# A four-layer graph network on one core: layer 2 in 128-row groups written out, layer 0 without zeroed weight buffers

## The chip, the cores and the metric

The kernel runs on one core of one Trainium2 chip. The metric is the device time of one execution in microseconds; three runs of the kernel before gave a median of 2008.88 us (2003.04 to 2011.71).

## What is computed

3125 nodes with 256 features, 53125 edges sorted by destination (25000 random pairs in both directions and a loop on every node). Four layers, each followed by a residual and a layer norm over the features:

```python
edge_index = jnp.stack([src, dst])
x = _layernorm(x + _L0_gnn_ref(x, edge_index, W, b), axis=-1)                  # relu(sum of h[src] * dinv[src] * dinv[dst] + b), h = x @ W
x = _layernorm(x + _L1_gnn_ref(x, edge_index, edge_weight, ...), axis=-1)      # (sum of x[src] * w) @ W_rel.T + b_rel + x @ W_root.T
x = _layernorm(x + _L2_gnn_ref(x, W, att, src, dst), axis=-1)                  # attention, 4 heads of 64
x = _layernorm(x + _L3_gnn_ref(x, edge_weight, W, b, src, dst), axis=-1)       # relu(sum of (x @ W)[src] * w + b)
```

Layer 2 in full:

```python
z = jnp.einsum('nd,hdf->nhf', h, W)
es = jnp.einsum('nhf,hf->nh', z, a_src)
ed = jnp.einsum('nhf,hf->nh', z, a_dst)
e = jax.nn.leaky_relu(es[src] + ed[dst], SLOPE)
e = jnp.where(e == 0.0, NEG, e)
m = jax.ops.segment_max(e, dst, num_segments=N)
ex = jnp.exp(e - m[dst])
denom = jax.ops.segment_sum(ex, dst, num_segments=N)
alpha = ex / safe
out = jax.ops.segment_sum(alpha[:, :, None] * z[src], dst, num_segments=N)
```

## The kernel before, in words

Nodes lie in 25 tiles of 128. The kernel is written engine by engine: each of SP, POOL (GpSimd), ACT, DVE and PE has its own list of instructions, and semaphores with counts set the order between them.

**Start.** SP loads destinations, sources and weights of the edges, x and the matrices, and last the destinations once more in the grouping of layer 2 (dst_i, L310). DVE packs the edges into a table of six bf16 fields; SP stores it in DRAM (edge_list, L313) and spreads it to overlapping rows (edge_rows, L317). DVE also counts degrees, finds for each group of layer 2 its lowest node and, from the widest group, how many sweeps layer 2 needs (nsw, one here); TensorE's first products of x wait for that (L742, L1119). ACT scales them (L471), once the edge list is stored, since the results take its place.

**Layer 0** also builds the adjacency matrices that layers 1 and 3 use. For every tile t of sources, 32 panels of destinations lie on 32 partitions with 128 edges each. POOL (edge_rows) gathers the panels' rows from edge_rows by an indirect DMA (L413), moves the cursor (L417) and marks edges of another panel (L419, L422). TensorE turns the five fields (turn_fields, L1144), ACT copies them in two halves (digits, L489), DVE makes one-hots of them (one_hot_lo L775, one_hot_code L778) and multiplies them by three bf16 parts of the weight (weighted, L783). TensorE makes from them, in eight quads (adjacency), counts (L1157) and weights (L1160). ACT evicts the counts (L493); DVE adds each quad of weights to the weight buffer aw[t % 2] (add_weights, L796). The buffer holds zeros before: POOL wrote them (L427) after the store of tile t-2 (a_stored), and DVE waits for that (c_zero). SP stores the finished buffer to DRAM (L324). Then TensorE multiplies the counts with the scaled features (aggregate, L1168), and the residual parts of the tiles before are done: sums0 (L812, L815), the norm (L800, L801, L498, L805, L806), the turning of the normalised tile (L1177) and the two products of layer 1 (L1186). The number of rounds per tile (nswb) is read at run time; it is one here. The program of one tile has the turning of the next fields between the fourth and the fifth quad. DVE makes the next tile's one-hots between its additions 4 to 7, in an order written out by hand.

**Layer 1** loads the stored matrices (four slots) and makes dense products (L1224), and the rows of the attention table: per node 268 floats, z with a one behind each head and both logits. SP stores them in DRAM (L346, L349).

**Layer 2** goes over groups of edges. A group is EP x KC = 125 x 5 edges: 85 groups, taken five at a time (SLOTS) in a loop of 17 turns; the first and the last turn are written out apart. Per group: SP loads the source indices (L361) once the slot of the ring is free, and the destination logits of a window of 48 nodes (L367); POOL gathers five times 125 rows of the attention table by indirect DMAs (L450), five groups ahead at most. DVE makes one-hots of the destinations within the window (L901, L906), TensorE turns them (L1255), multiplies them by the window's logits (L1264), DVE forms the logits (L912 to L931), masks them to the window (L938), takes the maximum over the five edges of a partition (L946); TensorE turns that (L1273), DVE takes the maximum over the partitions (L951), puts it on a diagonal (L957), TensorE spreads it to all partitions (L1281), DVE updates the running maximum (L966, L972, L982) and shifts the logits (L977), ACT takes the exponentials (L568, L571), TensorE sums the gathered rows by window (L1290, 40 small products a group), DVE rescales and adds (L990, L998). The parts of neighbouring groups are interleaved by hand: in one step DVE masks group k, prepares k+1 and k+2 and finishes k-1 and k-2. Windows start at a base that each engine loads into a register (base_i); a turn of the loop loads anew the bases of the groups that it touches.

**Layer 3** multiplies by its matrix (L1354) and makes the dense products with the stored matrices again.

## Time and profile before

| what | us |
|---|---|
| median of 3 runs | 2008.88 (2003.04 to 2011.71) |
| the profiled execution, its own time | 2004.1 |
| its span, first to last instruction | 2002.2 |
| around the span | 1.9 |
| TensorE busy | 1748.5 (87%) |
| DVE busy | 1274.0 (64%) |
| POOL busy | 673.2 (34%) |
| ACT busy | 449.5 (22%) |
| mean granted clock of TensorE | 0.81 of full speed |

A share of the whole span is an average over stages with different limits, so the stages are read one by one: layer 0 lasts from about 110 us to 615 us of the span, layer 1 to 940, layer 2 to 1631, layer 3 to the end. Instructions are named by their line of the kernel before; "idle before" names the time in which the engine stood still ahead of an instruction, and what ended it ("issue": nothing that the profile shows). PEld is TensorE's weight load, which overlaps its products.

### The profile page before, as it was taken

What the parts mean: (1) busy time and instruction counts of PE and PEld (TensorE: products, weight loads), DVE (VectorE), ACT (ScalarE), POOL (GpSimd) and SP (SyncE); (2) the same over time, 40 slices, a digit from 0 to 9 for tenths busy, and PEclk for the clock granted to TensorE, in tenths of its full rate; (3) what the DMA queues carried; (4) which work ended last, traced back from release to release, by engine and by line L of the source; (5) the groups of instructions that cost most, each with busy time, mean ns of one, the idle gap of its engine ahead of it and who ended that gap; (6) DMA issues with size and microseconds to landing.
All of it is one profiled execution on the core that took longest, in us unless ns stands there. A gap on an engine that the chain in (4) does not pass through costs nothing.

```text
span 2002.2 us, 38284 instructions
## 1 busy us (share of the span) xinstructions
PE 1748.5 (87%) x13533; PEld 1503.9 (75%) x13533; DVE 1274.0 (64%) x2915; ACT 449.5 (22%) x1000; POOL 673.2 (34%) x567
## 2 busy tenths in 40 slices
PE   5668898888888999996689889998988877899998
PEld 5457777767776888885578778887877765788887
DVE  9678888888885112222788888888898876311212
ACT  0432322222321001002233332332333333100000
POOL 0122222222222000001777777777777800000000
PEclk9989999999999999998555555555555555899999
DMA  6102121212124344441333333333333330245441
GB/s 168 70 36 102 70 102 70 102 70 102 70 103 197 108 143 143 151 146 45 91 91 83 89 86 88 86 85 89 86 89 88 90 114 1 97 151 176 162 157 45
DMA packets 110199, 202.38 MB, mean 101 GB/s; under 512 B 70372, under 2 KB 87061, under 8 KB 100483
## 3 DMA queue, kind: packets, MB, share of 16 engines
q1 hardware_dynamic: 54851, 141.62, 20.1%
q0 software_dynamic: 55232, 59.15, 12.3%
q8 instruction: 80, 1.31, 0.3%
q14 instruction: 36, 0.29, 0.0%
HBM read 152.00 MB, written 53.36 MB: 103 GB/s over the span
## 4 chain that ended last, share of the span: by engine, by line
PE 57%; issue 23%; DVE 8%; DMA 4%; POOL 4%; ACT 2%; DVEq 1%; POOLq 0%; SPq 0%; ACTq 0%
PE bank L1224 27%; PE bank L1290 16%; PE bank L1281 4%; DMA ring<-edge_rows,cur 3%; PE bank L1264 2%; PE bank L1354 2%; POOL ring L450 2%; PE bank L1273 1%; PE bank L1232 1%; POOL ring L419 1%; DVE work L957 1%; PE bank L1177 1%; PE bank L1337 1%; ACT ring L593 1%; DMA ring<-attention_rows,work 1%
## 5 line engine op out<-in xcount | busy, mean ns | idle before, releaser
L450 POOL DMA_INDIRECT ring<-attention_rows,work x425 | 514.8, 1211 | 172.9 <-issue 143.4
L1290 PE MATMUL bank<-work,ring 125*65 125x48 f32 x3400 | 395.1, 302 | 0.0
L1290 PEld LDWEIGHTS bank<-work,ring 125*65 125x65 f32 x3400 | 387.7, 224 | 8.4
L1224 PE MATMUL bank<-big,ring 128*128 128x256 f32 x1250 | 273.0, 379 | 1.4 <-DVE x_sb L821 1.4
L1224 PE MATMUL bank<-big 128*128 128x256 f32 x1250 | 272.9, 379 | 0.0
L1224 PEld LDWEIGHTS bank<-big,ring 128*128 128x128 f32 x1250 | 236.5, 190 | 33.8 <-DVE x_sb L821 2.2
L1224 PEld LDWEIGHTS bank<-big 128*128 128x128 f32 x1250 | 236.6, 190 | 31.7
L1168 PE MATMUL bank<-big 128*128 128x256 bf16 x1875 | 209.0, 273 | 14.6 <-ACT big L493 14.6
L1168 PEld LDWEIGHTS bank<-big 128*128 128x128 bf16 x1875 | 181.4, 98 | 38.9 <-ACT big L493 18.3
L427 POOL MEMSET big<- 128x3200 f32 x25 | 69.2, 2770 | 355.3 <-DMA adjacency<-big 295.2
L1157 PE MATMUL bank<-work 128*128 128x100 bf16 x800 | 153.5, 210 | 33.4 <-DVE big L796 28.8
L1160 PE MATMUL bank<-work 128*128 128x100 bf16 x2400 | 164.5, 210 | 0.0
L1160 PEld LDWEIGHTS bank<-work 128*128 128x128 bf16 x2400 | 151.1, 99 | 0.2
L946 DVE TENSOR_REDUCE work<-work 125x192 f32<-125x960 f32 x85 | 150.9, 1776 | 0.0
L783 DVE TENSOR_TENSOR work<-work,ring 128x1600 bf16<-128x1600 bf16 x156 | 149.3, 985 | 0.0
L498 ACT ACTIVATE std<-mv,epsc 128x1 f32<-128x1 f32 x100 | 29.5, 295 | 527.7 <-DVE mv L801 527.7
L1281 PE MATMUL bank<-work,ones 96*128 96x192 f32 x170 | 82.7, 588 | 72.9 <-DVE work L957 72.9
L1053 DVE TENSOR_TENSOR u<-bank,bias 128x256 f32<-128x256 f32 x25 | 10.6, 424 | 211.1 <-PE bank L1224 211.1
L796 DVE TENSOR_TENSOR big<-big,bank 128x400 f32<-128x400 f32 x200 | 113.4, 567 | 23.5 <-PE bank L1160 23.4
L493 ACT CAST big<-bank 128x400 bf16<-128x400 f32 x200 | 98.5, 492 | 120.9 <-PE bank L1160 120.9
L1157 PEld LDWEIGHTS bank<-work 128*128 128x128 bf16 x800 | 78.7, 98 | 44.9 <-DVE big L796 36.0
L1281 PEld LDWEIGHTS bank<-work,ones 96*128 96x128 f32 x170 | 41.2, 301 | 94.0 <-DVE work L957 94.0
(204 smaller groups left out, 2153.8 us busy)
## 6 DMA issues: line engine op xcount, KB each, us to landing
adjacency<-big SPq DMA_DIRECT2D x25, 1600.0 KB, 5.2
ring<-adjacency SPq DMA_DIRECT2D x25, 1600.0 KB, 7.0
big<-adjacency SPq DMA_DIRECT2D x25, 1600.0 KB, 7.2
ring<-attention_rows,work POOLq DMA_INDIRECT x425, 3.9
edge_rows<-edge_list SPq DMA_DIRECT2D x1, 4983.0 KB
x_sb<-in_x SPq DMA_DIRECT2D x1, 3072.0 KB
out_x<-xnT SPq DMA_DIRECT2D x24, 128.0 KB, 4.3
attention_rows<-ring SPq DMA_DIRECT2D x13, 135.0 KB, 2.3
```

The source lines that it names most:

```text
L427: G.memset(aw[t % 2], 0.0).then_inc(c_zero, 1)
L450: G.indirect_dma_start(out=rows[0:EP, s, c, 0:ZG], out_offset=None, in_=ztab[:, :], in_offset=bass.IndirectOffsetOnAxis(ap=idx[:, s, c:c + ...
L493: S.copy(ac[:, :, q * QUAD * PAN:(q + 1) * QUAD * PAN], cnt_banks[q % 2][:, 0:NT * QUAD * PAN].rearrange("p (b d) -> p b d", b=NT)).then_i ...
L783: ins = V.tensor_tensor(oh[h][2][:, j], oh[h][1], repeated(digs[h][:, W1 + j], NT * PAN), ALU.mult)
L796: V.tensor_tensor(part, part, w_banks[q % 2][:, 0:NT * QUAD * PAN].rearrange("p (b d) -> p b d", b=NT), ALU.add).then_inc(c_wad, 1)
L946: V.tensor_reduce(vmax[:], val[:, three(s)].rearrange("p c w -> p w c"), AX_X, ALU.max).then_inc(y["vmax_ready"], 1)
L1157: mm(cnt_banks[b][:, 0:NT * QUAD * PAN].rearrange("p (b d) -> p b d", b=NT)[:, :, cols], lo[:, g, :, m], code[:, g, :, m].rearrange("p (b ...
L1160: ins = mm(w_banks[b][:, 0:NT * QUAD * PAN].rearrange("p (b d) -> p b d", b=NT)[:, :, cols], lo[:, g, :, m], wtd[:, j, g, :, m].rearrange( ...
L1168: ins = mm(out_banks[t % 2][:, 0:D], ac[:, b, :], y0p[:, b, j, :], start=False, stop=False, skip_group_check=True)
L1224: ins = mm(bank[:, 0:D], slots[s][:, b, :], ybuf[:, b, :], start=(b == 0), stop=(b == NT - 1))
L1281: mm(mb_bank[:, 0:HW], ones[0:2 * WIN, :], dg[:].rearrange("p k w -> p (k w)"), start=True, stop=True).then_inc(y["mb"], 1)
L1290: ins = mm(sum_banks[three(s)][0:FH, h * WIN:(h + 1) * WIN], rows[0:EP, s, c, h * FH:(h + 1) * FH], prob[:, s % 2, c, h * WIN:(h + 1) * WI ...
```

## The change

Layer 0: POOL zeroes the two weight buffers once (t < 2) and no more. Every addition is a scalar_tensor_tensor: old content times a column of keep, plus the new quad; the column is 0 for the first round of a tile and 1 for others. DVE, and no more POOL, waits for the store of the buffer two tiles back. Addition 5 stands ahead of one_hot_lo, and the later additions and products move accordingly.

Layer 2: groups have 128 x 5 = 640 edges. 83 are full, the 84th has the last five edges; its empty rows have a destination of 1e30, no one-hot, and source 0, and the search for bases and sweeps ignores them (a few more DVE operations). No loop over turns: all 84 groups are written out on all five engines, and buffers that went by slot % 2 with an exception for the fifth go by group number % 3 and % 2. SP copies all source indices at the start from DRAM to DRAM into the layout of the groups (source_nodes) and loads them at once in layer 1, ahead of the fourth matrix; POOL waits for that one load and for the slot. SP has the window loads only.

```diff
@@ sizes @@
-    EP = max(p for p in range(1, P + 1) if E % (p * KC * SLOTS) == 0)
-    GROUPS = E // (EP * KC)
-    TURNS = GROUPS // SLOTS
+    EP = P
+    FULL = E // (EP * KC)
+    GROUPS = FULL + 1
+    REST = (E - FULL * EP * KC) // KC
@@ SP, start @@
-            sp.dma_start(dst_i[:], dst.rearrange("(g p k) -> p g k", p=EP, k=KC)).then_inc(ld_dsti, 16)
+            sp.dma_start(dst_i[:, 0:FULL, :], dst[0:FULL * EP * KC].rearrange("(g p k) -> p g k", p=EP, k=KC)).then_inc(
+                ld_dsti, 16)
+            sp.dma_start(dst_i[0:REST, FULL, :], dst[FULL * EP * KC:E].rearrange("(p k) -> p k", k=KC)).then_inc(ld_dsti, 16)
+            sp.dma_start(src_all[:, 0:FULL, :], src[0:FULL * EP * KC].rearrange("(g p k) -> p g k", p=EP, k=KC)).then_inc(
+                s_srcs, 16)
+            sp.dma_start(src_all[0:REST, FULL, :], src[FULL * EP * KC:E].rearrange("(p k) -> p k", k=KC)).then_inc(s_srcs, 16)
+            sp.dma_start(src_all[REST:EP, FULL, :], spare[REST:EP, :]).then_inc(s_srcs, 16)
@@ SP, layer 1 @@
+                elif t == 3:
+                    sp.wait_ge(s_srcs, 48)
+                    sp.wait_ge(c_quad, nswb * (QUADS * NT))
+                    sp.sem_inc(held, 1)
+                    sp.dma_start(idx, src_all).then_inc(idx_ready, 16)
@@ SP, layer 2 @@
-                with sp.Fori(0, TURNS) as q:
-                    for s in range(SLOTS):
-                        i = r * GROUPS + q * SLOTS + s
-                        sp.wait_ge(y["slot_free"], i + 1)
-                        sp.dma_start(idx[:, s, :], src_v[:, bass.ds(q * SLOTS + s, 1), :].rearrange(
-                            "p a k -> p (a k)")).then_inc(idx_ready[s], 16)
-                        sp.wait_ge(z_stored[0], 16 * (NT - NT // 2))
-                        sp.wait_ge(z_stored[1], 16 * (NT // 2))
-                        base = sp.value_load(base_i[0:1, bass.ds(q * SLOTS + s, 1)], min_val=0, max_val=NPAD - WIN)
-                        sp.wait_ge(y["ed_ps"], i + 1)
-                        sp.dma_start(edw[:, s, :], ztab[bass.ds(base, WIN), ED:ZG]).then_inc(edw_loaded[s], 16)
+                for g in range(GROUPS):
+                    s = g % SLOTS
+                    base = sp.value_load(base_i[0:1, g:g + 1], min_val=0, max_val=NPAD - WIN)
+                    sp.wait_ge(y["ed_ps"], r * GROUPS + (g + 1))
+                    sp.dma_start(edw[:, s, :], ztab[bass.ds(base, WIN), ED:ZG]).then_inc(edw_loaded[s], 16)
@@ POOL, layer 0 @@
-                if t >= 2:
-                    pool.wait_ge(a_stored[t % 2], 16 * (t // 2))
-                G.memset(aw[t % 2], 0.0).then_inc(c_zero, 1)
+                if t < 2:
+                    G.memset(aw[t % 2], 0.0).then_inc(c_zero, 1)
@@ POOL, layer 2 @@
+            pool.wait_ge(idx_ready, 16)
             with pool.Fori(0, nsw) as r:
-                with pool.Fori(0, TURNS) as q:
-                    for s in range(SLOTS):
-                        pool.wait_ge(idx_ready[s], 16 * (r * TURNS + q + 1))
-                        pool.sem_inc(held, 1)
+                for g in range(GROUPS):
+                    s = g % SLOTS
+                    pool.wait_ge(y["slot_free"], r * GROUPS + (g + 1))
+                    pool.sem_inc(held, 1)
@@ DVE, start @@
-            dve.wait_ge(ld_dsti, 16)
-            link(V.tensor_copy(dstf[:], dst_i[:]))
+            dve.wait_ge(ld_dsti, 32)
+            V.tensor_copy(dstf[:, 0:FULL, :], dst_i[:, 0:FULL, :])
+            link(V.tensor_copy(dstf[0:REST, FULL, :], dst_i[0:REST, FULL, :]))
             V.tensor_reduce(gmin[:], dstf[:], AX_X, ALU.min)
-            V.tensor_reduce(gmax[:], dstf[:], AX_X, ALU.max).then_inc(s_gm, 1)
+            link(V.scalar_tensor_tensor(out=within, in0=dstf[:], scalar=BIG / 2, in1=dstf[:], op0=ALU.is_lt, op1=ALU.mult))
+            link(V.tensor_scalar(gmin[:], gmin[:], float(N), None, ALU.min))
+            V.tensor_reduce(gmax[:], within, AX_X, ALU.max).then_inc(s_gm, 1)
@@ DVE, layer 0 @@
-                V.tensor_tensor(part, part, w_banks[q % 2][:, 0:NT * QUAD * PAN].rearrange("p (b d) -> p b d", b=NT),
-                                ALU.add).then_inc(c_wad, 1)
+                V.scalar_tensor_tensor(out=part, in0=part, scalar=keep[:, bass.ds(r, 1)],
+                                       in1=w_banks[q % 2][:, 0:NT * QUAD * PAN].rearrange("p (b d) -> p b d", b=NT),
+                                       op0=ALU.mult, op1=ALU.add).then_inc(c_wad, 1)
-                    dve.wait_ge(c_zero, t + 1)
+                    if t < 2:
+                        dve.wait_ge(c_zero, t + 1)
+                    else:
+                        dve.wait_ge(a_stored[t % 2], 16 * (t // 2))
-                        add_weights(t, i, 4)
+                        add_weights(t, i, 4, r)
+                        add_weights(t, i, 5, r)
                         one_hot_lo(0)
-                        add_weights(t, i, 5)
+                        add_weights(t, i, 6, r)
                         weighted(i + 1, 0, 0)
-                        add_weights(t, i, 6)
-                        weighted(i + 1, 0, 1)
-                        add_weights(t, i, 7)
-                        weighted(i + 1, 0, 2)
+                        add_weights(t, i, 7, r)
+                        for j in range(1, 3):
+                            weighted(i + 1, 0, j)
@@ DVE, layer 2; ACT and PE alike @@
-                attention_turn(r, 0, first=True)
-                with dve.Fori(1, TURNS - 1) as q:
-                    attention_turn(r, q)
-                attention_turn(r, TURNS - 1, last=True)
+                attention(r)
```

## Rows read from the trace of the kernel before

**Rows 1.** Chain that ended last, 100 to 600 us: two of 24 gathers' landings.

```profile
139.13 2.38 DMA ring<-edge_rows,cur
...
580.90 2.38 DMA ring<-edge_rows,cur
```

**Rows 2.** Timeline of a tile of layer 0: start us, us, engine, line, idle before it.

```profile
197.22 2.76 POOL L427 MEMSET big<- 128x3200 f32 x1 [13.15 <-DMA adjacency<-big]
...
198.90 1.22 DVE L806 TENSOR_SCALAR x_sb<-u,mv,rstd 128x256 f32<-128x256 f32 x1
...
204.04 0.49 ACT L493 CAST big<-bank 128x400 bf16<-128x400 f32 x1 [0.24 <-PE bank L1160]
...
204.72 0.37 PE L1144 MATMUL bank<-ident,ring 32*128 32x32 bf16 x5 [0.72 <-POOL ring L422]
...
205.57 0.99 DVE L778 TENSOR_TENSOR work<-ring 128x1600 bf16<-128x1600 bf16 x1 [0.96 <-ACT ring L489]
...
219.17 0.51 DVE L806 TENSOR_SCALAR x_sb<-u,mv,rstd 128x256 f32<-128x256 f32 x1
```

**Rows 3.** TensorE's waits, 100 to 600 us (waited for: us in total, times, longest us).

```profile
PE bank L1144 <- POOL ring L422: 18.8, 23, 2.4
```

**Rows 4.** Timeline of layer 2, two periods from 1308.80 us.

```profile
1308.80 0.30 PEld L1273 LDWEIGHTS bank<-ident,work 125*96 125x96 f32 x2
...
1316.58 0.30 PEld L1273 LDWEIGHTS bank<-ident,work 125*96 125x96 f32 x2
...
1318.39 0.35 DVE L990 TENSOR_TENSOR big<-big,work 65x192 f32 x1 [0.54 <-issue]
...
1325.00 0.31 PEld L1273 LDWEIGHTS bank<-ident,work 125*96 125x96 f32 x2
```

**Rows 5.** Busy us by stage: PE, PEld, DVE, ACT, POOL, granted clock, DMA share, GB/s.

```profile
1300.00:1500.00 200.00, 179.20 (x1385) 159.02 (x1385) 173.73 (x440) 62.66 (x103) 154.62 (x128) 0.53 0.38 87
```

**Rows 6.** Timeline of the start of layer 2.

```profile
937.19 0.33 SPq L349 DMA_DIRECT2D attention_rows<-ring  x1
...
945.16 1.29 POOL L450 DMA_INDIRECT ring<-attention_rows,work  x1 [25.18 <-issue]
...
955.84 0.17 DVE L918 TENSOR_TENSOR work<-ring,bank 125x20 f32<-125x20 f32 x1 [8.79 <-DMA ring<-attention_rows,work]
...
971.00 1.21 POOL L450 DMA_INDIRECT ring<-attention_rows,work  x1 [0.31 <-issue]
```

**Rows 7.** DVE by line: count, busy us, mean ns, idle before.

```profile
L876 DVE TENSOR_TENSOR u<-bank,x_sb 128x256 f32<-128x256 f32 x25 | 10.4, 417 | 19.8 <-PE bank L1224 19.8
L812 DVE SCALAR_TENSOR_TENSOR u<-bank,dinv,bias 128x256 f32<-128x256 f32 x25 | 11.9, 476 | 0.0
```

**Rows 8.** Timeline of DVE in tile 0, 109 to 136 us.

```profile
112.56 1.22 DVE L775 TENSOR_TENSOR work<-ring 128x2048 bf16<-128x2048 bf16 x1
...
113.69 2.79 DVE L783 TENSOR_TENSOR work<-work,ring 128x1600 bf16<-128x1600 bf16 x3
...
117.30 1.38 DVE L775 TENSOR_TENSOR work<-ring 128x2048 bf16<-128x2048 bf16 x1
...
118.60 3.05 DVE L783 TENSOR_TENSOR work<-work,ring 128x1600 bf16<-128x1600 bf16 x3
```

**Rows 9.** POOL by line: its two gathers, of 125 rows and of 32, and two operations.

```profile
L450 POOL DMA_INDIRECT ring<-attention_rows,work x425 | 514.8, 1211 | 172.9 <-issue 143.4 <-DMA work<-in_src 29.5
...
L413 POOL DMA_INDIRECT ring<-edge_rows,cur x26 | 24.7, 951 | 44.4 <-PE bank L1144 38.6 <-issue 5.7
...
L419 POOL TENSOR_SCALAR ring<-ring,panel 32x128 bf16<-32x128 int16 x26 | 22.1, 851 | 2.3
...
L422 POOL TENSOR_TENSOR ring<-ring 32x128 bf16<-32x128 bf16 x26 | 16.6, 639 | 2.2
```

**Rows 10.** Timeline of the start: the edge list's issue and ACT's first scaling.

```profile
22.25 16.87 SPq L313 DMA_DIRECT2D edge_list<-big  x1
...
64.42 0.47 ACT L471 ACTIVATE u<-bank,dinv 128x256 f32<-128x256 f32 x1 [2.95 <-PE bank L1130]
```

184 lines of the change are left out of this document (83 added, 101 removed).

## The prediction, made before the change was run

> **What bounds the kernel now.** I read the busy time by stage first, then for each stage that the change touches the waits, one repeated stretch of the timeline, and the chain that ended last. Two stages are touched: layer 0 (about 110 to 615 us, 25 tiles) and layer 2 (about 940 to 1631 us, 85 groups). Layers 1 and 3 aren't: there TensorE runs dense products back to back.
>
> Layer 0. A tile takes 20.08 us: from the gather of edge rows at 139.13 to the one at 580.90 there are 22 tiles [rows 1]. The chain alternates between engines. In the tile shown [rows 2] DVE ends the normalisation L806 at 200.12 (198.90 + 1.22); TensorE then turns x and makes four quads of the adjacency; ACT evicts the fourth until 204.53; TensorE could turn the next fields but waits 0.72 us for POOL's L422; ACT copies the digits, and DVE starts the one-hot L778 at 205.57. From there DVE has no gap until the next L806 ends at 219.68 but for one wait of 0.36 on a square root. So 5.45 + 14.11 = 19.56 us: DVE binds the long part, and POOL's lateness delays its start. POOL is late since it zeroes the weight buffer (L427, 2.77 us) behind a wait for the store of that buffer, and the gather is queued behind. TensorE waited 18.8 us for L422 in 23 tiles [rows 3]. The zeroing does a second harm: L806 takes 1.22 us at 198.90, under L427 (197.22 to 199.98), and 0.51 at 219.17, where it runs out [rows 2].
>
> Layer 2. The period is read at TensorE's transposes L1273: 1308.80 to 1316.58 is 7.78 us, and 1316.58 to 1325.00 is 8.42 [rows 4]. The long one comes once per turn of the loop over five groups; the other four are 7.79. In it DVE's L990 stands 0.54 us at "issue", when a fresh turn loads window bases again. Within a period the chain goes L1273, DVE's group maximum and diagonal (about 1.9 us), then L1281 and 40 small products back to back until the next L1273. TensorE is busy 179.2 of 200 us, at a mean granted clock of 0.53, so mostly at the lower of its two levels (1.2 GHz) [rows 5]. POOL is close behind: from 945.16 to 971.00 it started 17 more gathers, 1.52 us each, so 7.60 per group [rows 6].
>
> **Layer 0, the change priced.** Zeroing goes for tiles 2 to 24, and with it POOL's wait for the store. DVE now waits for that store itself, at the start of tile t for the store of tile t-2. The store was POOL's releaser at 197.22 at the latest, a few us before the next tile's first addition and about a tile before DVE needs it, so this costs nothing. POOL's gather for the next tile now starts as soon as TensorE has turned the last fields, half a tile or more early: POOL's lateness is gone. What is late next is the eviction by ACT: the digits can be copied from 204.53, and L778 follows 0.36 us behind (as 205.22, the copy, to 205.57), so at 204.89. The stretch from L806 to L778 falls from 5.45 to 4.77.
> The additions gain a scalar read from SBUF. Its price is the difference of L876 (no scalar) and L812 (a scalar column), both 256 columns with a PSUM operand: 476 - 417 = 59 ns an addition [rows 7]. Four of eight lie in DVE's long stretch, and the first delays a quad: +0.3 a tile. Its bounds are 0 and 0.5 (all eight).
> The new order puts addition 5 right behind 4, so TensorE waits less for it ahead of its eighth quad. TensorE isn't last there any more (without the wait for POOL its own cycle is 19.56 - 0.72 = 18.8 or less, under DVE's below), so this is slack, priced at nothing.
> That gives 4.77 + 14.11 + 0.3 = 19.2. Against it stands a collision. POOL's three small operations per tile ran beside DVE's additions; now they come right behind the turning of the fields and fall on DVE's bf16 one-hots. Tile 0 already has that order: there DVE's L775 took 1.38 us for 1.22, and a run of three L783 3.05, where an undisturbed run takes 2.79 [rows 8]. So DVE loses up to 0.42 a tile. I take half, 0.2, since in later tiles additions with a PSUM operand lie between. Period 19.4, gain 0.68 in 23 tiles, 15.6, and about 2.4 more in tile 1, whose fields came latest: 18 us. The bounds are 8 (full collision, 0.5 for the additions) and 26 (neither).
> **Layer 2, the change priced.** 128 rows to a group give 83 full groups and one of five edges: 84 for 85, and the last costs as much as a full one. One group less: -7.8. The loop over turns is written out and bases are loaded once each: 16 passages from one turn to the next at 8.42 - 7.79 = 0.63: -10. Partitions cost no time in DVE's and ACT's operations; what grows is the free size of the transposes (125 to 128 columns) and of the maximum over them (250 to 256): about 0.016 + 0.006 + 0.012 us on the chain, by 3/125 of 0.65, 3% of 0.42 and 3/125 of 0.6: +3 over all.
> Indices. Before, SP loaded them per group behind a wait for the slot, and POOL's first gather stood behind that at 945.16, though the last rows of the attention table were sent at 937.19 [rows 6]. Now all lie ready; POOL starts when that store has landed (2.3 us later by the median of these stores) at about 939.9: -5.3 at the head, where DVE waits for gathered rows (8.79 us at 955.84). The one load of all indices sits in SP's queue in layer 1 ahead of a load of adjacency that is needed a tile later: nothing. SP's window loads lose the slot wait ahead of them: nothing, they are early.
> A gather of 128 rows: 32 rows took 951 ns, 125 take 1211 [rows 9], so 3 rows more are about 0.01 us and a group is 5 x 1.53 = 7.65. Below 7.82, so still hidden, by 0.17 a group only. If each group's wait costs POOL 0.15 us more, both are level; the bound is 0 to +8 us over all.
> Sum: -7.8 - 10 + 3 - 5.3 = -20. Bounds -28 and -10.
>
> **Start.** SP gets five small transfers for one (the last group apart, and source indices copied within DRAM in pieces of 20 bytes, as many as the destination load has, 10,624). They stand ahead of the edge list. Before, SP's issue of the edge list stood 16.87 us behind the destination load [rows 10]. A second such copy delays the edge list by about 17 us, twice that at most. What hides it: ACT's first scaling, which needs the list stored, came at 64.42, some 22 us after the store had landed (39.1 + 2.6); POOL's first gather needs the rows made from it, about 21 us later still, and its fields are turned at 110 only. So 17 us cost nothing, 34 would cost 12.
> The Trainium skill, DMA: Bandwidth & Descriptors, Specifications, has transfers under 512 bytes done as read-modify-write, which speaks for the longer end; no row here writes such pieces to DRAM in number.
> DVE's extra work before the sweeps are known (a product of 420 columns like the reductions beside it, 0.6, and three small ones) lies on the path to the first matmul of x: +1. The extra memsets lie in DVE's wait for the first indices.
>
> **The sum.** -18 - 20 + 1 = -37 on the profiled execution's 2004.1 us: 1967. That execution is 4.8 us below the median of 2008.88, so the forecast of the median is **1971 us**.
>
> **Rivals.**
> A. DVE stands still for POOL's operations in full, as L806 did under L427. L419 and L422 are 0.85 + 0.64 = 1.5 us a tile [rows 9], the period 19.2 + 1.5 = 20.7, layer 0 is 23 x 0.6 - 2.4 = 12 us slower than before instead of 18 faster, the whole 2001. For: L806. Against: tile 0, where DVE lost 0.42. Chance 0.07.
> B. TensorE gets the upper clock level in layer 2, since the long gaps of the turns are gone. Then POOL binds: 7.65 for 7.82, 84 x 0.17 = 14 less, so 1957, and if its gathers are a little shorter 1950. For: the chain is denser. Against: it is at the lower level in nearly all of the stretch though busy 0.9 of it [rows 5]. Chance 0.15.
> C. Slower: POOL becomes the bound of layer 2. Its 420 gathers then set the time: 84 x 5 x (g + 0.31), g the gather. With g = 1.22 that is 643 and hidden; layer 2's gain is gone at g about 1.28, and the whole kernel is slower than before from g = 1.33, 9% above 1.22. At g = 1.40 it is 420 x 0.07 = 29 us slower: 2038. For: POOL is only 0.17 us a group from the bound. Against: the slope from 32 to 125 rows. Chance 0.04.
> D. The written-out code stalls at instruction fetch in layer 2, on DVE or TensorE: the 10 us of the turns don't come back and some are added: 1985. For: four engines now stream new code for 650 us. Against: layers 1 and 3 are written out and show even steps. Chance 0.08.
> E. The change doesn't do as said: a group of 640 edges spans over 48 nodes, and all groups are swept twice, over 600 us more. The mean degree is 17, a group spans 38 nodes; in the sorted indices of the reference's input the widest has 41. Left out.
>
> **Chances and range.** Forecast (1960 to 1984) 0.66, A 0.07, B 0.15, C 0.04, D 0.08. The range takes in B, D and the bounds of the two stages together (2009 + 1 - 28 - 26 = 1956 and 2009 + 1 - 10 - 8 = 1992), and at the low end B with short gathers: 1948 to 1992. A and C, and what nobody thought of, lie outside. About 0.5% (10 us) is what a measurement of this kernel tells from no change: faster by more than that 0.89 (the forecast, B, D), within it 0.07 (A), slower 0.04 (C).
>
> **What would show it.** In the changed profile: 84 executions of L946's operation, steps of 7.8 us with no long one in five; the first gather of layer 2 near 940 on the old scale; no wait of TensorE for POOL in layer 0; tiles of 19.4 us, L806's operation at 0.41 to 0.51 throughout; additions longer by 0.06 us. The collision is read at the one-hots' mean (985 ns) and its spread, rival C at POOL's mean and at waits of DVE for gathered rows, D at "issue" in layer 2, the start at the time of ACT's first scaling. I am wrong if tiles stay at 20 us, or if layer 2's step is over 7.9.

## The result, and the profile after

The changed kernel takes 1934.26 us (median of 4 runs, 1933.84 to 1938.50) where the one before takes 2007.1 (4 runs, 2003.04 to 2011.71): a ratio of 0.9641, 95% interval 0.9615 to 0.9667, so 73 us less. The prediction was 1971 with a range of 1948 to 1992: right in its sign, wrong in its size, and the time lies outside the range. The profiled execution after took 1934.25 us, its span is 1932.4 (before: 2004.1 and 2002.2); the spans differ by 69.8 us.

The page of the kernel after (line, engine, operation, shapes, count | busy us, mean ns | idle before):

```profile
span 1932.4 us, 37246 instructions
PE 1671.7 (87%) x13479; PEld 1430.2 (74%) x13479; DVE 1273.7 (66%) x2904; ACT 446.0 (23%) x996; POOL 625.3 (32%) x539
...
L463 POOL DMA_INDIRECT ring<-attention_rows,work x420 | 397.4, 946 | 224.0 <-issue 134.2
...
L793 DVE TENSOR_TENSOR work<-work,ring 128x1600 bf16<-128x1600 bf16 x156 | 149.1, 995 | 0.0
...
L806 DVE SCALAR_TENSOR_TENSOR big<-big,ring,bank 128x400 f32<-128x400 f32 x200 | 122.9, 626 | 36.2 <-PE bank L1159 33.9
...
L435 POOL TENSOR_TENSOR ring<-ring 32x128 bf16<-32x128 bf16 x26 | 123.9, 4764 | 2.2
```

Three marks on the time axis cut the difference up. Timelines of the kernel after (start us, us, engine line, operation): the turning of the fields for the first tile and for the last passage of layer 0, and the maximum over a group's edges for the first and the last group of layer 2.

```profile
124.70 0.38 PE L1143 MATMUL bank<-ident,ring 32*128 32x32 bf16 x5 [3.12 <-DVE big L778]
...
598.82 0.36 PE L1143 MATMUL bank<-ident,ring 32*128 32x32 bf16 x4
...
944.20 1.81 DVE L958 TENSOR_REDUCE work<-work 128x192 f32<-128x960 f32 x1
...
1546.17 1.84 DVE L958 TENSOR_REDUCE work<-work 128x192 f32<-128x960 f32 x1
```

The same four of the kernel before:

```profile
110.97 0.39 PE L1144 MATMUL bank<-ident,ring 32*128 32x32 bf16 x5 [3.12 <-DVE big L768]
...
604.62 0.40 PE L1144 MATMUL bank<-ident,ring 32*128 32x32 bf16 x5
...
957.90 1.76 DVE L946 TENSOR_REDUCE work<-work 125x192 f32<-125x960 f32 x1
...
1615.62 1.78 DVE L946 TENSOR_REDUCE work<-work 125x192 f32<-125x960 f32 x1
```

| stretch | before | after | difference | predicted |
|---|---|---|---|---|
| start, to the first turned fields | 110.97 | 124.70 | +13.7 | +1 |
| layer 0, first to last turned fields | 493.65 | 474.12 | -19.5 | -18 |
| layer 1 and the head of layer 2 | 353.28 | 345.38 | -7.9 | -5.3 |
| layer 2, first to last group | 657.72 | 601.97 | -55.7 | -15 |
| what follows | 386.6 | 386.2 | -0.4 | 0 |

The sum is -69.8. Layer 0 came as predicted, the start cost more, and layer 2 gave nearly four times what was expected. A step of layer 2 is counted from one group's maximum (L946, now L958) to the next. There were 84 of a mean of 7.83 us and are 83 of 7.25. In the kernel after nearly all are of two kinds; the expectations call a step at the lower clock level cold and one at the upper level warm. The timeline of the kernel after shows both, first one at TensorE's lower clock level, then one at the upper:

```profile
1350.22 0.21 PEld L1263 LDWEIGHTS bank<-work 48*128 48x128 bf16 x5
...
1353.67 0.30 PEld L1272 LDWEIGHTS bank<-ident,work 128*96 128x96 f32 x2
...
1354.45 0.43 DVE L963 TENSOR_REDUCE bank<-bank 96x2 f32<-96x256 f32 x1 [0.60 <-PE bank L1272]
...
1357.91 3.37 PEld L1289 LDWEIGHTS bank<-work,ring 128*65 128x65 f32 x30
...
1361.14 0.30 PEld L1272 LDWEIGHTS bank<-ident,work 128*96 128x96 f32 x2
...
1437.80 1.85 PEld L1289 LDWEIGHTS bank<-work,ring 128*65 128x65 f32 x30
...
1438.17 1.84 DVE L958 TENSOR_REDUCE work<-work 128x192 f32<-128x960 f32 x1
...
1440.06 0.17 PEld L1272 LDWEIGHTS bank<-ident,work 128*96 128x96 f32 x2 [0.41 <-DVE work L958]
...
1443.22 0.30 PEld L1280 LDWEIGHTS bank<-work,ones 96*128 96x128 f32 x2 [2.22 <-DVE work L969]
...
1444.90 1.83 DVE L958 TENSOR_REDUCE work<-work 128x192 f32<-128x960 f32 x1
```

From L1272 to L1272 the first is 7.47 us (1353.67 to 1361.14), where [rows 4] had 7.78, and no long one stands in five any more. In the second the 30 loads of L1289 take 1.85 instead of 3.37, TensorE waits 2.22 us for VectorE's L969, and the step from L958 to L958 is 6.73 (1438.17 to 1444.90). VectorE has no gap in it, so VectorE sets it. Steps under 7 us number 23 of 83 after and 4 of 84 before. The granted clock says the same. The stages of both kernels between 980 and 1540 us (busy PE, PEld, DVE, ACT, POOL, then the clock, the DMA share and GB/s), before:

```profile
980.00:1540.00 560.00, 503.46 (x3874) 447.98 (x3873) 484.26 (x1211) 172.68 (x285) 432.62 (x358) 0.53 0.38 88
```

and after:

```profile
980.00:1540.00 560.00, 472.29 (x4163) 415.23 (x4164) 526.70 (x1311) 186.22 (x308) 362.52 (x384) 0.62 0.37 97
```

The first load of the first kind of step leads further. It belongs to the products of the destination logits: five loads of the transposed one-hots, 48 rows by 125 columns before and by 128 after. A line of before's timeline and the group of instructions by shape, before:

```profile
1312.73 0.60 PEld L1264 LDWEIGHTS bank<-work 48*125 48x125 bf16 x5
...
L1264 PEld LDWEIGHTS bank<-work 48*125 48x125 bf16 x425 | 49.7, 210 | 11.1 <-issue 4.2
```

and after:

```profile
L1263 PEld LDWEIGHTS bank<-work 48*128 48x128 bf16 x420 | 16.9, 100 | 10.6 <-issue 4.2
```

In a step at the lower level the five together took 0.60 us before and take 0.21 after (0.12 and 0.04 a load; the means of one, 210 and 100 ns, are longer since neighbouring loads overlap), and with their products 0.69 and 0.29. There are more columns, and they take a third of the time. The Trainium skill, TensorE: Matmul & The Clock Gate, section Weight-path perf modes — Fast Weight Load (FWL) and DoubleRow, has a fast load that is on "when the number of weights is 128 and the input dtype is not FP32"; this is bfloat16, and the trace agrees.

A second thing became cheaper: a gather of layer 2 takes 946 ns where it took 1211 [rows 9].

### The profile page after: what moved, and what is told of

Read it like the earlier page. It is cut to its first block, busy times and chain, and to the rows that moved or that the text cites. A ratio compares the mean times of both kernels' runs of the same rounds, so it can differ in the third digit from the quotient of the medians.

```text
span 1932.4 us, 37246 instructions
## 1 busy us (share of the span) xinstructions
PE 1671.7 (87%) x13479; PEld 1430.2 (74%) x13479; DVE 1273.7 (66%) x2904; ACT 446.0 (23%) x996; POOL 625.3 (32%) x539
## 3 DMA queue, kind: packets, MB, share of 16 engines
q0 software_dynamic: 20992, 59.37, 11.6%
## 4 chain that ended last, share of the span: by engine, by line
PE 72%; DVE 12%; issue 8%; SPq 3%; ACT 3%; DVEq 1%; DMA 1%; POOL 0%; ACTq 0%; POOLq 0%
PE bank L1223 28%; PE bank L1289 15%; PE bank L1167 10%; PE bank L1159 4%; PE bank L1280 3%; PE bank L1345 2%; PE bank L1185 2%; PE bank L1156 2%; DVE big L806 2%; SPq L322 2%; PE bank L1272 1%; DVE work L988 1%; PE bank L1176 1%; PE bank L1231 1%; DVE work L969 1%
## 5 line engine op out<-in xcount | busy, mean ns | idle before, releaser
L463 POOL DMA_INDIRECT ring<-attention_rows,work x420 | 397.4, 946 | 224.0 <-issue 134.2
L1289 PE MATMUL bank<-work,ring 128*65 128x48 f32 x3360 | 361.7, 289 | 0.0
L1289 PEld LDWEIGHTS bank<-work,ring 128*65 128x65 f32 x3360 | 354.0, 209 | 7.7
L958 DVE TENSOR_REDUCE work<-work 128x192 f32<-128x960 f32 x84 | 154.0, 1833 | 0.0
L1159 PEld LDWEIGHTS bank<-work 128*128 128x128 bf16 x2400 | 151.8, 99 | 0.1
L1280 PE MATMUL bank<-work,ones 96*128 96x192 f32 x168 | 75.5, 547 | 86.7 <-DVE work L969 86.7
L793 DVE TENSOR_TENSOR work<-work,ring 128x1600 bf16<-128x1600 bf16 x156 | 149.1, 995 | 0.0
L806 DVE SCALAR_TENSOR_TENSOR big<-big,ring,bank 128x400 f32<-128x400 f32 x200 | 122.9, 626 | 36.2 <-PE bank L1159 33.9
L435 POOL TENSOR_TENSOR ring<-ring 32x128 bf16<-32x128 bf16 x26 | 123.9, 4764 | 2.2
L1280 PEld LDWEIGHTS bank<-work,ones 96*128 96x128 f32 x168 | 37.6, 279 | 105.6 <-DVE work L969 105.6
L426 POOL DMA_INDIRECT ring<-edge_rows,cur x26 | 37.0, 1424 | 231.3 <-PE bank L1143 231.2
```

The source lines that it names most:

```text
L435: G.tensor_tensor(raw[:, :, CODE], raw[:, :, CODE], off, ALU.add).then_inc(c_raw, 1)
L463: G.indirect_dma_start(out=rows[0:EP, s, c, 0:ZG], out_offset=None, in_=ztab[:, :], in_offset=bass.IndirectOffsetOnAxis(ap=idx[:, g, c:c + ...
L793: ins = V.tensor_tensor(oh[h][2][:, j], oh[h][1], repeated(digs[h][:, W1 + j], NT * PAN), ALU.mult)
L806: V.scalar_tensor_tensor(out=part, in0=part, scalar=keep[:, bass.ds(r, 1)], in1=w_banks[q % 2][:, 0:NT * QUAD * PAN].rearrange("p (b d) -> ...
L958: V.tensor_reduce(vmax[:], val[:, k % 3].rearrange("p c w -> p w c"), AX_X, ALU.max).then_inc(y["vmax_ready"], 1)
L1159: ins = mm(w_banks[b][:, 0:NT * QUAD * PAN].rearrange("p (b d) -> p b d", b=NT)[:, :, cols], lo[:, g, :, m], wtd[:, j, g, :, m].rearrange( ...
```

## The experiments

The theory: layer 2's gain beyond the forecast is the fast load first, then more steps at the upper clock level. The rivals: the gathers, the loops written out, or the group less. Each run is set beside runs of before on its own chip: mostly two chips that take 2008 to 2009 us for it, once one of 2019. One more chip, on which four of the runs below were made, takes 2082 us for it; it is called the slow chip. No profile of before was kept on it, but that of the change of layer 0 alone was: there its layer 2 lasts 734.8 us from the first to the last group's maximum, on the chip of 2019 us 671.0, and its layer 0 is about as long on both (471.9 and 473.7).

**128 columns of weights, and nothing else.** In the kernel before:

```diff
-        hotT = carve(WIN, KC, EP, dt=BF16)
+        hotT = carve(WIN, KC, P, dt=BF16)
-                S.copy(hotT[:], hotT_bank[:, :, 0:EP])
+                S.copy(hotT[:, :, 0:EP], hotT_bank[:, :, 0:EP])
+            V.memset(hotT[:, :, EP:P], 0.0)
-                ins = mm(ed_bank[0:EP, ...], hotT[:, c, :], ...)
+                ins = mm(ed_bank[0:P, ...], hotT[:, c, :], ...)
```

> The kernel before with one edit: the transposed one-hots are 128 columns wide, the last three of them zero, so that the products of destination_logits load 128 columns of weights where they loaded 125. Groups stay 125 edges, the gathers stay 125 rows, and everything else is as before. Theory FAST LOAD (a load of bfloat16 weights is several times shorter with 128 columns than with 125): a load falls from about 0.12 to 0.04 us, the five products and loads of a group from some 0.69 to 0.29 us, a cold step of layer 2 from 7.8 to about 7.5; over 85 groups less the warm ones some 20 to 30 us, so a time of 1977 to 1987 us. Rival BY COLUMNS (a load costs in proportion to its columns, as my prediction had it): +3 columns in 125 are worth less than 0.1 us in a group, so 2007 us, within 2 us of before. Rival GATHER (layer 2 became shorter because the gathers of 128 rows are): no change here either, since they stay at 1.21 us.

Measured: 1987.46 us against 2008.81, ratio 0.9893 (0.9876 to 0.9910), so 21 less, just above the fast load's 1977 to 1987. Layer 2 went from 657.7 to 637.5 us, its plain step from 7.79 to 7.40. Groups by shape:

```profile
L1265 PEld LDWEIGHTS bank<-work 48*128 48x128 bf16 x425 | 17.4, 102 | 11.2 <-issue 4.2
```

**127 columns.** The same edit with P - 1 in place of P.

> The kernel before with one-hots of 127 columns (two zero) where the run that gave 1987 us had 128 and the kernel before has 125. Theory THRESHOLD AT 128: five loads of the destination logits stay at 0.60 us, the cold step at 7.79, and the time at 2005 to 2012. Rival BY COLUMNS above some number under 128: the loads fall to 0.21 us and the time to 1984 to 1991.

Measured: 2008.08 us against 2008.07, ratio 0.9999 (0.9985 to 1.0013). Nothing:

```profile
L1265 PEld LDWEIGHTS bank<-work 48*127 48x127 bf16 x425 | 49.2, 206 | 11.0 <-issue 4.2
```

So of the three widths run, 125, 127 and 128, only the last is fast: the price jumps between 127 and 128 and does not slope with the columns.

**128 rows in a gather, and nothing else.** In the kernel before, with the three last indices zero and their rows unused:

```diff
-        idx = carve(EP, SLOTS, KC, dt=I32)
+        idx = carve(P, SLOTS, KC, dt=I32)
-                                out=rows[0:EP, s, c, 0:ZG], ...
+                                out=rows[0:P, s, c, 0:ZG], ...
```

> The kernel before with one edit: each gather of layer 2 fetches 128 rows (the last three indices are zero and their rows are used by nothing) where it fetched 125. Groups, products and the index loads stay as before. The mean of a gather should fall from 1.211 to about 0.95 us whatever the theory. Theory FAST LOAD (PE sets layer 2's step, and its loads got shorter): POOL is hidden except at the head of the layer, so 2007 less about 1 to 4 us: 2003 to 2006. Rival GATHER (POOL's 6.3 us a group and the DMA queue's time stood in the way of VectorE's wait for gathered rows and so of the step): a good part of layer 2's gain appears here, 15 to 35 us, so 1972 to 1992.

Measured: 1999.9 us against 2008.81, ratio 0.9962 (0.9949 to 0.9974): 5 to 10 us less. That is more than the 1 to 4 that I gave it under the fast load and less than the rival's 15. The page:

```profile
L450 POOL DMA_INDIRECT ring<-attention_rows,work x425 | 402.6, 947 | 273.9 <-DMA work<-in_src 165.4
```

The gather went from 1211 to 947 ns, and the queue's packets from 55,232 to 21,232 for the same 59 to 60 MB. The first group's maximum follows the first gather by 10.15 us instead of 12.74 (959.11 less 948.96; 957.90 less 945.16). Within layer 2 the plain step stayed at 7.79, but 13 steps of 84 are under 7.3 us where 5 were, and the layer is 7.8 us shorter (657.7 to 649.9). The Trainium skill, DMA: Bandwidth & Descriptors, section Why a DMA increments its semaphore by 16 and not by 1, says that a transfer is spread over the largest number of engines, up to 16, that divides the slowest dimension of both its sides: 5 for 125 rows, 16 for 128. The fall in packets and the time agree; the trace does not show by itself which engines took part.

**The kernel after with groups of 125.** Written out and with all indices loaded at once, but 85 groups of 125 rows:

```diff
-    EP = P
-    FULL = E // (EP * KC)
+    EP = 125
+    FULL = E // (EP * KC) - 1
```

> The kernel after with groups of 125 rows (85 groups of 5 x 125, written out, all indices loaded at once): layer 0 and the start of the kernel after, the row count of before. Theory FAST LOAD with its parts added up: a cold step goes back from 7.47 to about 7.8, one group more (7.8), gathers back at 1.21 us; 0.32 x 83 + 7.8 + about 2 for the head of the layer gives 1934 + 36 = 1970, and the steps at the ends of the turns of five stay gone. Rival LOOPS (most of the 56 us came from the loops written out, the row count was worth one group only): 1934 + 8 to 12 = 1942 to 1946. My prediction put the row count at one group less (-7.8) and wider operands (+3), so it would say 1939.

Measured: 2007.73 us against 2008.81 for before, and 73 more than the kernel after: beyond even the larger expectation. Two thirds are layer 2, 969.58 to 1620.16 = 650.6 us, 49 more than after, its plain step again 7.79 with no long one in five. So writing the turns out, with the indices loaded at once, is worth 7.1 us within the layer (657.7 to 650.6), near the 10 predicted. The rest is the start, as its timeline shows:

```profile
22.17 17.17 SPq L319 DMA_DIRECT2D big<-in_dst  x1
...
40.36 49.79 SPq L322 DMA_DIRECT2D source_nodes<-in_src  x1
```

L319 loads the last group's destinations and L322 copies its sources. Both are small; the transfer of 10,500 pieces of 20 bytes stands just ahead of each, and its own issue is short (0.94 us for L320, the copy). So the time shows at the issue behind the large transfer. In the kernel after, with 10,624 pieces over 128 rows, the same two lines take 8.38 and 31.07 us. The fields' first turn comes at 146.41 us, 21.7 later than in the kernel after. Whoever lays out indices over 125 rows pays at the queue, too.

**Both widenings in the kernel before.** The edits of the first and third run together. On the chip whose layer 2 is slow:

> The kernel before with both widenings and nothing else: one-hots of 128 columns (three of them zero) and gathers of 128 rows (three of them unused). Still 85 groups of 125, loops of five. By itself the first gave 1987 and the second 2000 (before 2009). Theory SUM (the two act apart: the load in PE's cold step, the gather at the layer's head and through a few more steps at the upper clock): -21 and -9 make about 1979, with the cold step at 7.40 us. Theory CLOCK BY DMA (the upper clock comes more often in layer 2 where the gathers' queue carries fewer packets and PE has shorter loads together, which the kernel after had): some 20 steps of 6.7 us instead of 5 to 10, and 1968 to 1973. Rival OVERLAP (both remove the same wait): no better than 1986.

It took 2168.0 us there, ratio 1.0407, with steps of 9.1 to 10.3 us. VectorE stood 237 us in waits whose releaser the trace gives as "remote", and TensorE 236 us in waits for VectorE's L957; what that chip does I did not find out. On another chip:

> The kernel before with 128-column one-hots and 128-row gathers (three columns and three rows unused) again: on the slower chip it took 2168 us, 86 more than before, which neither of the two edits did alone on the first chip. Theory SUM: on a chip like the first, 1979 us, cold steps of 7.40. Theory CLOCK BY DMA: 1968 to 1973. Rival TOGETHER THEY HURT (short loads and short gathers in loops of five, with the small index and window loads between, disturb each other, whatever the chip): above 2009, with steps of over 9 us.

Measured: 1973.73 us against 2008.15, ratio 0.9828 (0.9812 to 0.9845), so 34 less, where the two singly gave 21 and 9. That the two hurt each other holds on one chip only. The time is near that of CLOCK BY DMA, but its mechanism is not there: 5 steps of 84 are under 7.3 us, not 20. Most of what came on top is in the two steps where one turn passes into the next: with wide weights alone they mostly took 7.8 and 7.8 to 7.9 us, with both 7.81 and 7.62, the plain ones 7.40 in both.

**Both widenings in written-out groups of 125.** First on the slow chip:

> The groups of 125 edges in 85 written-out groups, as in the run with groups of 125 rows, but with one-hots of 128 columns (three zero) and gathers of 128 rows (three unused). Against that run (2007.7 us) it tells what the two thresholds are worth without the loops; against the kernel after it tells what is left for one group less and for products over 128 rows. The source copy should stay as slow as there if its rows stay 125, some 22 us later than in the kernel after. Theory SUM: cold steps of 7.40 instead of 7.79 give 0.39 x 80 = 31, the head 2.6, and 1973 without more warm steps. Theory CLOCK (a written-out stream with short loads and short gathers gets the upper clock in some 24 of its steps as the kernel after does): some 11 to 13 us more off, 1960 to 1963. Rival PRODUCTS (the kernel after gained from its 128-row operands in the sums too): a cold step stays above 7.5 here and the time above 1980.

There it took 2049.55 us, steps of 8.16. Then again:

> 85 written-out groups of 125 with 128-column one-hots and 128-row gathers again (2050 us on the slower chip, its steps 8.16 there as those of 128-row groups were). On a chip like the first: theory SUM 1973 us with cold steps of 7.40; theory CLOCK 1960 to 1963, with some 24 steps of 6.7; rival PRODUCTS above 1980, cold steps above 7.5.

Measured: 1971.04 us against 2008.15, ratio 0.9814 (0.9798 to 0.9831). Layer 2 took 621.4 us, 29.2 less than in the run with 125 rows, and the start gave 5.4 (fields' first turn at 140.98 us for 146.41). The time is that of theory SUM (1973). The plain step is 7.47 as in the kernel after, and only 8 of 84 are under 7 us; the window from 980 to 1540 us:

```profile
980.00:1540.00 560.00, 500.31 (x4087) 441.89 (x4087) 514.82 (x1282) 182.59 (x302) 360.84 (x382) 0.54 0.36 96
```

So neither short loads nor short gathers nor code without loops bring the kernel after's 0.62.

**Sums over 128 rows.** The same, with three rows of the probabilities zero and the sums' products over all 128:

```diff
-        prob = carve(EP, 2, KC, HW)
+        prob = carve(P, 2, KC, HW)
-    mm(sum_banks[...], rows[0:EP, s, c, ...], prob[:, k % 2, c, ...])
+    mm(sum_banks[...], rows[0:P, s, c, ...], prob[:, k % 2, c, ...])
```

> As the run with 85 written-out groups of 125, 128-column one-hots and 128-row gathers (1971 us, layer 2 621 us from its first to its last group, 8 of 84 steps under 7 us, granted clock 0.54), with one more edit: the products of the sums run over 128 rows (three rows of the probabilities are zero) instead of 125. Theory ROWS (the sums' weight loads of 65 columns over 128 rows, or PE's whole activity over 128 rows, bring the upper clock more often): 16 to 22 steps under 7 us, a granted clock near 0.60, 8 to 12 us less: 1959 to 1963. Rival NOT THE ROWS (the number of warm steps has another cause, such as where in time layer 2 begins, or the vector engines' 128-row operands): 1969 to 1972, and 5 to 11 warm steps. Rival COST (three more rows cost time): above 1973.

Measured: 1962.88 us against 2008.07, ratio 0.9773 (0.9748 to 0.9798), 8 less than without. Layer 2 took 615.1 us; 15 steps are under 7 us. The window:

```profile
980.00:1540.00 560.00, 486.94 (x4137) 429.76 (x4138) 518.29 (x1297) 184.20 (x305) 363.66 (x385) 0.58 0.36 97
```

The time is in the 1959 to 1963 of theory ROWS and well below the 1969 of its rival; the steps and the clock fall just short of what ROWS had (16, and 0.60). Filling the last three rows of products that last as long as before goes with more steps at the upper level. The two runs were made on two chips, the one without on a chip that gives the kernel after 20 such steps, this one on the chip that gives the run with indices in four parts 23, the count of the kernel after's first profile; so some 3 of the 7 more steps may be the chip's. The time is not: before takes 2008.15 and 2008.07 us on the two. And the granted clock over the whole execution is 0.805 to 0.808 in all four executions without the rows and 0.818 to 0.821 in all four with them. That the edit brings a higher clock and 8 us is shown as far as two such chips can be compared; why, and where the kernel after's remaining 5 to 8 steps come from, is not.

**The change of layer 0 alone** in the kernel before. On the slow chip:

> The kernel before with the change of layer 0 alone: POOL zeroes the two weight buffers once, the additions scale the old content (by 0 on a tile's first passage), in the new order of VectorE. Start, layer 2 and its loops are those of before. Theory OF THE PREDICTION (the tile's period is VectorE's, 20.08 to 19.4 us, and POOL's zeroing was partly in its way): 18 to 20 us less, 1987 to 1991, with the POOL operation on the codes of the edge rows rising from 0.64 to some 6.8 us and nobody waiting for it. Rival ELSEWHERE (part of the 19.5 us that the field turns gained in the kernel after comes from the start's later edge list, not from the tiles): 5 to 12 us less, 1996 to 2003.

2062.14 us against 2082.43, ratio 0.9901 (0.9865 to 0.9936); from the first to the last turned fields 471.9 us, where the run with both widenings, whose layer 0 is that of before, took 495.7 on the same chip. On a chip whose before takes 2018.6 us:

> The change of layer 0 alone in the kernel before, again (2062 against 2082 us for before on the slower chip, field turns from first to last 471.9 instead of 493.7 us). On a chip like the first, theory OF THE PREDICTION: 18 to 22 us less than before, 1986 to 1990, layer 2 at its old 650 to 660 us. Rival: layer 2 takes part of it back through fewer steps at the upper clock, 1991 to 1997.

1998.98 us, ratio 0.9887 (0.9860 to 0.9914), so 23 less, give or take 5 (20 by the medians); 473.7 us in layer 0 (111.78 to 585.43). Both agree with the prediction's theory as to layer 0: the gain is in the tiles. The absolute time is above both ranges, and layer 2 took 671.0 us, not 650 to 660; no profile of before from this chip says what its layer 2 was without the change, so that layer 2 took a part back is not excluded by it.

**The source indices laid out later.** The two transfers of the copy behind the one that lays out the edge rows:

```diff
-            sp.dma_start(src_all[:, 0:FULL, :], src[0:FULL * EP * KC]...)
-            sp.dma_start(src_all[0:REST, FULL, :], ...)
             ...
             sp.dma_start(etab[:, :], ...).then_inc(s_etab, 16)
+            sp.dma_start(src_all[:, 0:FULL, :], src[0:FULL * EP * KC]...)
+            sp.dma_start(src_all[0:REST, FULL, :], ...)
```

> The kernel after with the two transfers that copy the source indices (L319's successors L320 and L322 of the profile after) placed behind the transfer that lays out the rows of edges; the small one that fills the last rows with zeros stays ahead of it. Theory QUEUE (SyncE's 31 us of issuing the copy delay the edge list and so the first field products by 13.7 us): POOL's first zeroing returns from 98.2 to about 85 us, the first turn of the fields from 124.7 to about 111, the time falls by 12 to 14 us: 1920 to 1922. Rival SHARED ENGINES (the copy's 10,624 pieces hold the DMA engines wherever they stand, and the transfers behind them, edge rows and weights, are late instead): the first turn of the fields falls by less than 4 us, or the first passages of layer 0 wait for their edge rows; 1930 to 1934.

2009.31 us on the slow chip (before 2082.43). Then beside the kernel after:

> The kernel after, unchanged, beside the three runs below on the same chip, because the last set of runs was made on a chip on which layer 2 is slower (before took 2082 us there, its layer 0 unchanged): if this chip is like the first, 1934 us; if it is like the last one, its layer 2 is slower by some 60 us and the time is about 2020 (the late copy took 2009 there).

> The late copy of the source indices again, beside the kernel after on the same chip. On the slower chip its fields' first turn came at 112.6 instead of 124.7 us and its layer 2 began 13.0 us earlier than in the kernel after. Theory QUEUE: 12 to 14 us less than the kernel after on this chip, 1920 to 1922 if it is 1934. Rival SHARED ENGINES: what the start gains is lost behind it, less than 4 us less.

Measured: the kernel after 1934.71, the late copy 1924.04 us, before 2008.15; ratios 0.9636 (0.9619 to 0.9652) and 0.9576 (0.9561 to 0.9592). So 10.7 less than the kernel after, nearly all of what theory QUEUE had (12 to 14), and the fastest kernel of the study. Timeline of the start, first SyncE's queue (L328 is the copy, L330 the small one behind it), then the fields' first turn:

```profile
31.18 2.09 SPq L323 DMA_DIRECT2D edge_list<-big  x1
...
37.80 13.05 SPq L328 DMA_DIRECT2D source_nodes<-in_src  x1
50.88 40.03 SPq L330 DMA_DIRECT2D source_nodes<-in_src  x1
...
113.11 0.38 PE L1143 MATMUL bank<-ident,ring 32*128 32x32 bf16 x5 [3.12 <-DVE big L778]
```

The copy now holds the queue for 53 us (37.80 to 90.91), and no other engine waits for SyncE in them.

**The indices loaded in four parts in layer 1**, straight from the input (only the last group, of five edges, keeps its copy):

```diff
                 load_a(slots1[s], t, a1_loaded[s])
+                if t in (3, 6, 9, 12):
+                    lo = (t - 3) // 3 * 21
+                    hi = min(FULL, lo + 21)
+                    sp.dma_start(idx[:, lo:hi, :], src[...]).then_inc(idx_ready, 16)
```

> The kernel after without its copy of the source indices to a second place in memory (but for the last group, of one edge): the indices are loaded straight from the input in four parts of 21 groups, behind the loads of adjacency tiles 3, 6, 9 and 12 of layer 1. The late copy gave 1924 against 1934.7. Theory QUEUE: the start is that of the kernel before (fields' first turn at 111 to 113 us), SyncE's four issues of some 8 to 10 us lie beside layer 1's products since tiles are loaded up to four ahead, and the time is 1920 to 1924. Rival LAYER 1 WAITS (a tile's load or a store behind such an issue comes late and PE waits for it, up to 8 us at each of the four): 1928 to 1950.

Measured: 1925.44 us against 2008.07, ratio 0.9589 (0.9562 to 0.9617): the late copy's time within the intervals. The fields' first turn came at 115.61 us, and from there to layer 2's first maximum it took 819.5 us, as in the kernel after, so nothing in layer 1 was late. Timeline of SyncE's queue around the second of the four:

```profile
666.43 0.43 SPq L362 DMA_DIRECT2D work<-in_src  x1
677.20 0.34 SPq L367 DMA_DIRECT2D attention_rows<-ring  x1
...
701.89 0.46 SPq L362 DMA_DIRECT2D work<-in_src  x1
```

Each of the four issues took 0.43 to 0.46 us. That is no price of the queue's time, though: at the start, too, the large transfers' own issues are short and the issue behind them is long, and here the next issue came 10 us or more later, so that a hold of the 8 to 10 us that I had put there would have run out unseen. What makes the 31 us at the start, the number of pieces, what is queued ahead of them, or memory as the place they go to, was not tested.

## Why the prediction was right or wrong

**Layer 0 was right, and so were its terms.** The addition was to grow by 59 ns, the difference of two rows: it went from 567 to 626. TensorE doesn't wait for POOL any more; its waits between 100 and 600 us begin (waited for: us in total, times, longest us):

```profile
PE bank L1167 <- ACT big L506: 14.0, 24, 0.6
PE bank L1156 <- DVE big L806: 13.7, 23, 2.7
```

and the 18.8 us for L422 [rows 3] are gone. From the fourth on, tiles take 19.1 to 19.5 us in the kernel after's two profiles for the forecast 19.4 (before 20.08 on average), the stretch 19.5 less for 18. The zeroing's second harm is gone as well. The normalisation by line between 110 and 600 us, before and after:

```profile
L806 DVE TENSOR_SCALAR x_sb<-u,mv,rstd 128x256 f32<-128x256 f32 x22 | 18.8, 855 | 0.8
...
L817 DVE TENSOR_SCALAR x_sb<-u,mv,rstd 128x256 f32<-128x256 f32 x23 | 9.5, 412 | 0.8
```

From there to layer 2's first maximum it is 7.9 less for the 5.3 predicted; 2.6 of them are the shorter gathers at the head.

**The collision went the other way.** "DVE stands still for POOL's operations in full" was rival A. VectorE's products of one-hots and weights (L783, now L793) rose by 1% only (985 to 995 ns), while POOL's L435 went from 639 ns [rows 9] to 4764 on average: 17 of the 26 take 6.8 us and the others 0.9 to 1.1. POOL's gather of 32 rows went from 951 to 1424 ns. It is POOL that stands still, and nobody waits for it since its gather is half a tile early. I had looked only for what the collision does to VectorE.

**The start: one step that failed is the cover,** the time that was said to hide the copy. The prediction had the copy at 17 us of the queue, "twice that at most", 17 hidden and 34 costing 12. The issue behind it took 31.07, and ScalarE's first scaling waited 10.59 us for the stored edge list, timelines of the kernel after:

```profile
22.07 8.38 SPq L319 DMA_DIRECT2D big<-in_dst  x1
30.50 2.37 SPq L320 DMA_DIRECT2D source_nodes<-in_src  x1
32.91 31.07 SPq L322 DMA_DIRECT2D source_nodes<-in_src  x1
...
64.47 2.97 SPq L326 DMA_DIRECT2D edge_list<-big  x1
...
77.10 0.47 ACT L484 ACTIVATE u<-bank,dinv 128x256 f32<-128x256 f32 x1 [10.59 <-DMA edge_list<-big]
```

It was at 64.42 [rows 10], so 12.7 later, and the first turned fields 13.7 (in the kernel after's second profile they come at 122.60, 11.6 later). I chose the near end from the one row of such pieces; the far end was the right one, and its price of 12 was right too. The sum should have carried it.

**Layer 2: the step that put the time outside the range is the term "wider operands, +3". It was mis-sized, and had the wrong sign.** The working was three columns in 125 more at the rate of the columns, for the transposes and the maximum alone. (Its three products come to 0.016, 0.013 and 0.014 us, so +3.6, and the whole sum to 1972 for 1971; neither matters.) That holds for the transposes (0.63 us over 128 columns, 0.62 over 125). The loads of L1264, whose columns grow by the same three, stood in the working nowhere, at nothing without a reason: the plain step became 0.39 us shorter by them in the loops, and 0.32 in the written-out code. (The 0.07 between lies ahead of L1280: VectorE's L934 takes 0.23 to 0.24 us there instead of 0.17. It does so only where wide operands and written-out code come together, 174 to 175 ns on average in the loops and in the run with 125 rows; why was not tested.) The runs give layer 2's 55.7 us by parts, each good to some 3 us since they were made on several chips: 657.7 before; 650.6 with the turns written out (-7.1, predicted -10); 621.4 with wide loads and gathers (-29.2, predicted about +3); 615.1 with 128-row sums (-6.3, not foreseen); 602.0 in the kernel after and 605.0 in its second profile (-10 to -13: a group less at 7.47, predicted -7.8, and 5 to 8 more steps at the upper level at 0.74 each).

**Rival B was half right.** "TensorE gets the upper clock level in layer 2" happened in a quarter of the steps, not in all. It said that POOL would bind there at 7.65 us a group; with gathers of 946 ns POOL needs 5 x 1.25 = 6.25, and VectorE binds at 6.7. The gather's price was another wrong reading of rows: I drew a line from 32 rows (951 ns) to 125 (1211) and set 128 on it, while in before's loops 32 and 128 rows cost the same (951 and 947 ns) and 125 is the exception. With that, C (POOL becomes the bound) had no ground.

**C and D did not happen.** VectorE's wait for gathered rows fell from 18.8 to 4.1 us over the layer, and no stall at "issue" grew in the code written out.

**The range failed since shorter loads had no rival.** The shorter plain step is 83 x 0.32 = 27 us, the 19 more steps at the upper level 19 x 0.74 = 14. Rival B had priced more of the upper level at 14 us and more, so that part had a place in the range. Without the shorter step the kernel would stand at 1961, inside the range, and without both at 1975. That 1975 is so near 1971 is partly luck: the start's unpriced 13 us and the turns' missing 3 stand against the gathers' gain at the head (2.6), 1.5 more in layer 0 and the +3 that was never paid.

## What to carry to other kernels

A size that becomes exactly 128 is not "three more": price it by rows that already have that size, not by a slope through smaller ones. In this kernel three columns of zeros, which widen the weights from 125 to 128, gave 21 us by one edit, and 127 gave nothing; going from 125 to 128 partitions cut a gather by 22% and the queue's time behind two transfers in small pieces by 51% and 38%. And a transfer that is "hidden" has to be priced at both ends of its time on the issuing queue, which shows at the issue behind it.

## What the runs showed of the hardware that was not expected

- Five loads of bfloat16 weights of 48 rows take 0.60 us at the lower clock level with 125 columns and 0.21 with 128; the mean of one over all steps is 210 ns with 125, 206 with 127, 100 with 128.
- A gather of rows of about 1.1 KB takes 1211 ns for 125 rows and 946 for 128; 55,232 packets became 20,992 for the same 59 MB.
- Beside VectorE's bfloat16 products a POOL operation on 32 x 128 elements takes 6.8 us in 17 of 26 tiles (4.8 on average) where it took 0.64, while VectorE loses 1%.
- Behind one DRAM-to-DRAM copy in 20-byte pieces the next issue on SyncE's queue took 31 us over 128 rows and 50 over 125; behind a load of as many pieces to SBUF it took 8.4 and 17.2. The large transfers' own issues took 0.3 to 2.4 us there.
- Products over 128 rows instead of 125 went with 15 instead of 8 steps at the upper clock level, a granted clock of 0.58 instead of 0.54, and 8 us less, on two chips that take the same time for the kernel before.
- The slow chip took 2082 us for the kernel before, and the kernel before with both widenings, 1.7% faster than before elsewhere, was 4.1% slower than before there.
